# Transposing four looked-up tiles at once, into the PSUM ring of the pieces

## The reference

```python
e = jnp.stack([tbl_0[ids[:, 0]], ..., tbl_31[ids[:, 31]]], axis=1)    # 1024 x 32 x 64
p, q = e[:, ROW], e[:, COL]                                            # ROW, COL: the 496 pairs
kp = jnp.einsum('bpj,ipj->bpi', p, kernel)                             # kernel: 64 x 496 x 64
z = jnp.sum(kp * q, axis=-1)
h = jnp.concatenate([z, dense_ctx], axis=1)
h = jnp.maximum(h @ W_top1 + b_top1, 0.0)                              # 512 x 512
h = jnp.maximum(h @ W_top2 + b_top2, 0.0)                              # 512 x 256
y = h @ W_top3
```

## Time and profile before

| | |
|---|---|
| median of 3 runs | 491.11 us |
| profiled execution | 495.24 us |
| its span, first to last instruction | 493.5 us |
| PE busy | 437.9 us, 89% |
| DVE busy | 301.4 us, 61% |
| ACT busy | 261.4 us, 53% |
| POOL busy | 231.6 us, 47% |
| mean granted TensorE clock | 0.965 |

### The profile page before, as it was taken

How to read it: one execution, slowest core, us unless ns; L and a number is a source line. 1 busy time by engine, 2 the same in 40 slices (tenths; PEclk the granted TensorE clock), 3 DMA queues, 4 the chain that set the end, 5 groups by cost and what they waited for, 6 DMA issues and landing times.

```text
span 493.5 us, 10180 instructions
## 1 busy us (share of the span) xinstructions
PE 437.9 (89%) x3421; PEld 263.6 (53%) x3421; DVE 301.4 (61%) x293; ACT 261.4 (53%) x1874; POOL 231.6 (47%) x251
## 2 busy tenths in 40 slices
PE   8859897978989799798989978987988979999997
PEld 5536464644655555456555645555654646664443
DVE  7407775776747756776666757675668767881000
ACT  6218755754646565645549655460875846601121
POOL 6456566655555645565556555555565530000000
PEclk9867999999999979999999989998999999999999
DMA  5525643121062100211121110301121101000000
GB/s 171 157 64 165 210 109 106 23 62 26 17 166 50 24 18 20 63 23 21 21 66 22 22 23 19 68 18 20 19 65 24 21 18 43 2 1 1 0 1 1
DMA packets 18266, 24.31 MB, mean 49 GB/s; under 512 B 6387, under 2 KB 11767, under 8 KB 17958
## 3 DMA queue, kind: packets, MB, share of 16 engines
q1 hardware_dynamic: 10406, 15.64, 10.8%
q0 software_dynamic: 7808, 8.01, 8.5%
HBM read 19.44 MB, written 0.00 MB: 39 GB/s over the span
## 4 chain that ended last, share of the span: by engine, by line
PE 73%; DVE 7%; another core or an unknown queue 7%; ACT 6%; issue 5%; POOL 0%; DVEq 0%; ACTq 0%; POOLq 0%
PE u_ps L693 30%; PE u_ps L714 12%; PE z_ps L727 10%; DVE prod L610 6%; PE u_ps L774 6%; PE z_ps L733 6%; ACT pass_prod L507 4%; PE t_ps L647 3%; PE u_ps L794 3%; PE u_ps L700 1%; DVE pass_prod L621 1%; PE z_ps L669 1%; ACT rows L495 1%; DVE prod L613 1%
## 5 line engine op out<-in xcount | busy, mean ns | idle before, releaser
L422 POOL DMA_INDIRECT nat<-tbl,ids_sb x244 | 230.5, 945 | 169.8 <-issue 63.0
L610 DVE TENSOR_TENSOR prod<-u_ps,rows 128x1024 f32<-128x1024 f32 x184 | 214.9, 1218 | 105.5 <-PE u_ps L693 71.9
L507 ACT ACTIVATE pass_prod<-pass_prod 128x64 f32<-128x64 f32 x896 | 214.5, 243 | 38.3 <-DVE pass_prod L621 26.5
L693 PE MATMUL u_ps<-rows,k_sb 64*128 64x256 f32 x1472 | 189.3, 395 | 26.8 <-DVE prod L610 10.6
L693 PEld LDWEIGHTS u_ps<-rows,k_sb 64*128 64x128 f32 x1472 | 138.7, 189 | 86.6 <-issue 38.4
L507 ACT ACTIVATION_READ_ACCUMULATOR pass_prod<-pass_prod 128x1 f32 x896 | 169.5, 189 | 2.5 <-issue 2.4
L621 DVE TENSOR_TENSOR pass_prod<-u_ps,nat 128x1024 f32<-128x1024 f32 x56 | 67.7, 1218 | 29.0 <-remote 13.7
L714 PE MATMUL u_ps<-k_sb,rows 64*128 64x256 f32 x448 | 70.0, 437 | 13.8 <-DVE prod L610 11.3
L495 ACT ACTIVATE rows<-t_ps 128x512 f32<-128x512 f32 (+1 forms) x38 | 19.6, 516 | 97.9 <-PE t_ps L647 43.0
L714 PEld LDWEIGHTS u_ps<-k_sb,rows 64*128 64x128 f32 x448 | 44.6, 208 | 34.3 <-DVE prod L610 21.0
L727 PE MATMUL z_ps<-prod,sel 128*32 128x512 f32 x512 | 62.6, 607 | 0.0
(11 more groups left out here) (50 smaller groups left out, 84.1 us busy)
## 6 DMA issues: line engine op xcount, KB each, us to landing
by_self<-rows SPq DMA_DIRECT2D x32, 128.0 KB
nat<-tbl,ids_sb POOLq DMA_INDIRECT x244
k_sb<-kern SPq DMA_DIRECT2D x3, 768.0 KB
k_sb<-kern SPq DMA_DIRECT2D x2, 640.0 KB
k_sb<-kern SPq DMA_DIRECT2D x1, 1152.0 KB
k_sb<-kern SPq DMA_DIRECT2D x2, 512.0 KB
rows<-w SPq DMA_DIRECT2D x1, 1024.0 KB
rows<-tbl SPq DMA_DIRECT2D x4, 224.0 KB
```

The costliest lines, as they stand in the source:

```text
L422: pool.indirect_dma_start(nat_of(m, n)[:, h * EMBED:(h + 1) * EMBED], None, tables[f], bass.IndirectOffsetOnAxis(ids_sb[:, col:col + 1], 0 ...
L507: op = nc.scalar.activation(of, of, ACT.Copy, accum_out=z_nat[:, b % 2, s, row:row + 1])
L610: nc.vector.tensor_tensor(to, u, by.unsqueeze(1).to_broadcast([P, 2, 2, SIZE]), ALU.mult).then_inc(prod_ready, 1)
L693: op = nc.tensor.matmul(u[:, h, :], k_sb[part, k_of(d), side, :], rows[part, tile, cols_of(b)], start=True, stop=True)
```

## The change

Tiles of block 1 and later are transposed four at a time. Their 1024 columns go into an item of the ring `u_ps`, in turn with the pieces (`RING_ITEMS`, `OF_PIECE`, `OF_TILES` hold who has which item); whoever takes an item waits for the one three items before it (`bank_free`), be that a product by DVE or a copy by ACT. ACT copies the four tiles by one instruction. Where a burst has quads and no fold, the four tiles come behind the quads on PE, and behind the copies of `z_ps` on ACT. The look-ups run up to 40 quarter tiles ahead, growing from tile 12 to tile 21. `fold` waits only for the 16 copies of block 0, since `t_ps` is used by nobody else afterwards.

```diff
-AHEAD = 30
+AHEAD, MORE_AHEAD = 30, 10
+def ahead(m):
+    return AHEAD + min(MORE_AHEAD, max(0, m - 11))
 def pieces_in_front(m):
-    return max(0, (4 * m - AHEAD) * (ND + NP) // (4 * TILES))
+    return max(0, (4 * m - ahead(m)) * (ND + NP) // (4 * TILES))
...
     def count(self):
         m = len(self.done)
-        return 2 if m >= TILES and m % 2 == 0 else 1
+        return 4 if m >= TILES else 1
...
+def behind_sums(n):
+    return len(PLAN.quads[n]) > 0 and PLAN.folded[n] is None
...
+RING_ITEMS, OF_PIECE, OF_TILES = [], [], {}
+def take_banks(looked_up):
+    for m, count in looked_up:
+        if m >= TILES:
+            OF_TILES[m] = len(RING_ITEMS)
+            RING_ITEMS.append((None, m + count))
+for n in range(PIECES):
+    take_banks(PLAN.before[n])
+    OF_PIECE.append(len(RING_ITEMS))
+    RING_ITEMS.append((n + 1, None))
+    take_banks(PLAN.behind[n])
...
+        def t_in_ring(m):
+            return u_ps[:, OF_TILES[m] % URING].rearrange("p h s n -> p (h s) n")
...
-                    nc.scalar.activation(rows[:, tile:tile + count, cols_of(b)],
-                                         t_ps[:, 0:count].rearrange("p t n c -> p t (n c)"), ACT.Copy).then_inc(rows_ready, count)
+                    nc.scalar.activation(rows[:, tile:tile + 4, cols_of(b)], t_in_ring(m), ACT.Copy).then_inc(rows_ready, 4)
...
+            def bank_free(item):
+                if item >= URING:
+                    piece, tiles = RING_ITEMS[item - URING]
+                    if piece is not None:
+                        pe.wait_ge(prod_ready, piece)
+                    else:
+                        pe.wait_ge(rows_ready, tiles)
...
+            def transpose_four(m):
+                for t in range(4):
+                    pe.wait_ge(gathered[(m + t) % LANES], lane_count(m + t))
+                bank_free(OF_TILES[m])
+                for t in range(4):
+                    for s in range(SUBS):
+                        op = nc.tensor.transpose(t_in_ring(m)[:, t, s * P:(s + 1) * P], nat_of(m + t, s), ident[:])
+                op.then_inc(transposed, 4)
...
-            def fold(b, tiles):
+            def fold(b):
...
-                pe.wait_ge(rows_ready, tiles)
+                pe.wait_ge(rows_ready, TILES)
...
             def interact(n, b, d):
-                if n >= URING:
-                    pe.wait_ge(prod_ready, n - URING + 1)
+                bank_free(OF_PIECE[n])
...
-                for m, count in PLAN.behind[n]:
-                    transpose(m, count, folds)
-                    tiles += count
+                if not behind_sums(n):
+                    for m, count in PLAN.behind[n]:
+                        if m >= TILES:
+                            transpose_four(m)
+                        else:
+                            transpose(m, count, folds)
+                        tiles += count
                 for quad in PLAN.quads[n]:
                     add_up(quad)
+                if behind_sums(n):
+                    for m, count in PLAN.behind[n]:
...
```

More of the change, by code:

```diff
@@ L170, in landed @@
                 continue
+            if pieces_in_front(n) >= len(self.through):
+                return float("inf")
             self.issued = max(self.issued, self.done[n - RING] if n >= RING else 0, self.through[pieces_in_front(n)]) + 2 * SUBS * GATHER
@@ L239, in in_front @@
         first, last = (next(mark[0] for mark in self.marks if mark[1] == n * (ND + NP)) for n in (1, BLOCKS))
-        due = first + (last - first) / (4 * (LOOKED_UP - TILES)) * (4 * (m - TILES) - AHEAD + part)
+        due = first + (last - first) / (4 * (LOOKED_UP - TILES)) * (4 * (m - TILES) - ahead(m) + part)
         return max(mark for mark in self.marks if mark[0] <= max(0, due))
@@ L291 @@
 PIECES = len(PLAN.order)
+def behind_sums(n):
+    return len(PLAN.quads[n]) > 0 and PLAN.folded[n] is None
 SELFS = [(b, d) for b, d, _ in PLAN.order if d is not None and DOUBLES[d][1] is None]
+assert all(m % 4 == 0 and count == 4 for looked_up in PLAN.before + PLAN.behind for m, count in looked_up if m >= TILES)
 assert PIECES == len(AT) == BLOCKS * (ND + NP) and PLAN.folds == BLOCKS
+RING_ITEMS, OF_PIECE, OF_TILES = [], [], {}
[9 more added lines that the diff above has]
+    take_banks(PLAN.behind[n])
 def tower(nc, ids, first_ids, tables, kern, dense, w1, b1, w2, b2, w3, out):
@@ L558, in _ @@
                     zT_evacuate(PLAN.folded[n])
+                if behind_sums(n):
+                    for m, count in PLAN.behind[n]:
+                        rows_out(m, count)
             z_evacuate(BLOCKS - 1, ZGROUPS - 1)
@@ L630, in _ @@
         def _(pe):
+            def bank_free(item):
[5 more added lines that the diff above has]
+                        pe.wait_ge(rows_ready, tiles)
             def fill(n, count):
-                if count and n >= URING:
-                    pe.wait_ge(prod_ready, n - URING + 1)
+                if count:
+                    bank_free(OF_PIECE[n])
                 for _ in range(count):
-                    nc.tensor.matmul(u_ps[:, n % URING, 0, 0, 0:P], ident[:], ident[:], start=True, stop=True)
+                    nc.tensor.matmul(u_ps[:, OF_PIECE[n] % URING, 0, 0, 0:P], ident[:], ident[:], start=True, stop=True)
             def transpose(m, count, folds):
@@ L713, in interact_pass @@
                         part = slice(EMBED * h, EMBED * (h + 1))
-                        op = nc.tensor.matmul(u_ps[:, n % URING, h, t, :], rows[part, first + t, at:at + P],
+                        op = nc.tensor.matmul(u_ps[:, OF_PIECE[n] % URING, h, t, :], rows[part, first + t, at:at + P],
                                               k_sb[part, k].rearrange("p s n -> p (s n)"), start=True, stop=True)
@@ L759, in _ @@
                     interact_pass(n, b, j)
-                for m, count in PLAN.behind[n]:
-                    transpose(m, count, folds)
-                    tiles += count
+                if not behind_sums(n):
+                    for m, count in PLAN.behind[n]:
+                        if m >= TILES:
+                            transpose_four(m)
+                        else:
+                            transpose(m, count, folds)
+                        tiles += count
                 for quad in PLAN.quads[n]:
                     add_up(quad)
+                if behind_sums(n):
+                    for m, count in PLAN.behind[n]:
+                        if m >= TILES:
+                            transpose_four(m)
+                        else:
+                            transpose(m, count, folds)
+                        tiles += count
                 if PLAN.folded[n] is not None:
-                    fold(PLAN.folded[n], tiles)
+                    fold(PLAN.folded[n])
                     folds += 1
```

16 lines of the change are left out of this document (9 added, 7 removed).

## The result

| | median of the runs, us | ratio to before |
|---|---|---|
| before (same chip) | 492.3 (489.6 to 494.8) | |
| the change | 511.0 (509.4 to 549.6) | 1.037 [1.033, 1.042] |

The change is 3.7% slower, about 18 us; the forecast was 490.5, and its range ended at 500.

What follows compares the result with a forecast made beforehand. The prediction took PE to bound the kernel, so only its idle time or work counts. Its terms, -5.5 + 4.3 + 0.6 + 0 = -0.6 us, lowered a median of 491.1 to 490.5 us, range 482 to 500 us.

Steps and rivals of the forecast that it cites:

- Look-ups: POOL's look-ups for groups of four, released further ahead: rows and ring places come in time, 0 us.
- Waits that come at the two groups right ahead of their pieces: Tiles 20 to 23 and 24 to 27: PE stands 1.26 us plus 0.9 us late signal each, +4.3 us.
- The nine groups behind the sums: Transposes behind the quads: two pieces cover the copy before the third piece needs its item, 0 us.
- the second rival: Slower: ACT, in its own pass sums, copies late and holds a ring item, delaying the third piece; 508 us, chance 0.15.
- the prediction's own sign: PE's waits for ACT's copies summing to over 8 us would show that ACT holds a ring item.
- Waits that go: PE's waits behind passes for two groups (1.67 and 3.54 us) and the second fold's 0.32 us vanish, together -5.5 us.
- The group ahead of its sums: Tiles 36 to 39 need a ring item after four doubles: zero in time, 1.1 us with late signal, +0.6 us.
- Transposes, copies, ACT's queue: As many transposes on PE, ACT's copies of 1.03 us off the path, its queued pass sums wanted later: 0 each.
- Faster, the delays go with the handovers: Half as many groups have half the late signals, halving PE's waits for DVE and ACT: -9.4 us, 482 us, chance 0.25.
- The clock falls at the two groups: Slower: transposes plus waiting at the groups right ahead of their pieces drop PE's clock, 3.2 us each; 497 us, chance 0.05.
- The rule of the Trainium skill on transposes: Transposes don't count as activity for PE's full clock, so eight in a row with a wait are one long pause.
- Look-ups too late for a group of four: Slower: look-ups come too late for a group of four tiles; no size given, chance 0.04.

Runs made afterwards that it cites:

- before_new_pace: The kernel before, with every look-up released where the change releases it (up to 40 quarter tiles ahead): 510.2 us, ratio 1.028.
- after_no_lookups: The change without the look-ups of tiles 20 to 63 and without the waits for them: 446.4 us, ratio 0.918.
- experiment 5: One memset ahead of each look-up from tile 8 on: in the change 508.1 us, in the kernel before with the change's release numbers 505.3 us.
- experiment 1: The kernel before with only the change's release numbers, 510.2 us (1.028); the change with before's numbers for tiles 2 to 19, 514.2 us (1.038).
- no_more_ahead: The change with look-ups released 30 quarter tiles ahead, without the ten more: 511.0 us, ratio 1.035.

## Why the prediction was wrong

**The step that failed** is *Look-ups*: "It fits: 0". It asked only whether the rows are there in time. They are, in the change. It never asked what ten look-ups more do to the signals of PE while they are issued, and it read the trace from 120 us on, where the transposes change, while the release numbers change from tile 7 on, in block 0. With before_new_pace this step measures +14 us (1.028), most of the loss. The forecast's own last sentence named the gap: it only carried the delays of PE's signals over. What it had seen, that they are late while look-ups run and in time after them, was right, and without look-ups DVE starts in time and PE never stands. It was told as a cost that is given, and not followed to what sets it: how closely look-ups follow one another, and for how long. The delay was also sized at PE's waits for DVE alone, 15.1 us; all that the 176 look-ups cost, with other waits, rows of matmuls that stretch and the clock, is 52 us.

**Waits that come at the two groups right ahead of their pieces, +4.3 us.** Right in kind, and a little too high. Without look-ups these waits are 1.27 and 1.26 us, the 1.26 of the sum. In the profiled execution of the change they are 1.26 and 1.27 too (L769 at 161.91, L749 at 182.59): the lower bound of 2.5 us, with no late signal at either.

**The nine groups behind the sums, 0.** Wrong for three of them even without look-ups. The working took the third piece behind a group as the first that needs it. Tiles 28 to 31 are needed by the next piece, tiles 40 to 43 and 56 to 59 by the second, and these three waits are 1.26 and twice 0.24 us in after_no_lookups. With look-ups a part of the second rival came true besides: in the trace of the change PE waits for a copy at six of the nine groups, 1.5 to 2.4 us each and 10.8 of the 12.1 us in all. By the prediction's own sign (over 8 us) the second rival would hold, and it had 17 us. But these waits lie beside waits for DVE: the change lies 2.7 us above the kernel with its release numbers in experiment 5 and 1.0372 - 1.028 = 0.9%, 4.5 us, in experiment 1 (2.0 us by the medians). Both differences are near the noise. So the groups cost some 2 to 5 us together, not 17.

**Waits that go, -5.5 us.** They went, and are inside these 2 to 5 us: the removed ones did not show as a gain of their own.

**The group ahead of its sums, +0.6.** Zero in the trace: PE goes from the burst to the transposes of tiles 36 to 39 without a gap.

**Transposes, copies, ACT's queue: 0.** Right in size: a copy of 1024 columns takes 1.02 us (estimated 1.03), and the eight transposes 1.0 us.

**Rivals.** *Faster, the delays go with the handovers*: refuted; half as many groups, and PE's waits for DVE rose to 18.6 us. *The clock falls at the two groups*: no run isolates transposes, but the clock was already lower where PE stood more, 0.89 instead of 0.93 in the first 120 us, before any group of four. The rule of the Trainium skill on transposes ("TensorE: Matmul & The Clock Gate", Part 4) changed nothing here: in after_no_lookups the stretches with groups of eight transposes keep a granted clock of 1.00. *Look-ups too late for a group of four* had 0.04; no_more_ahead shows that it was the reason for the ten look-ups more, 16.2 us of waits for rows. An upper bound of what look-ups may cost was never made; the rows for it were the earlier trace rows.

**What stays open.** Why a close row of look-ups delays PE's signals, and whether it is the signal that is late or PE's work (the ends of matmuls are modelled, and in the quads of 147.53 PE's own matmuls start late). Length of the pause, number of waits on POOL and pitch went together in the experiments (0.30 us, none and 1.25 us; 0.49, one and 1.43; 0.65, two and 1.60), so which of them lets a signal pass isn't told apart. How the price of k look-ups ahead grows with k, and what it is at the long pitch.

## What to carry to other kernels

A step that lets a producer run further ahead is not free because its results are in time: look at what issuing them does to everybody else, and begin to read where the release changes, not where the work does. Comparing the start of the same piece of work in two traces finds the place of a loss; the sums of waits from 120 us on pointed to the copies (8.4 us more), whose groups cost some 2 to 5 us in all. And leaving the suspected transfers out altogether is the first experiment to make, since it gives the size of the whole (52 us here) before its parts are argued.

## What the runs showed that I had not expected

- Indirect look-ups issued by POOL 1.25 us apart come with signals of PE that DVE, ACT and POOL see 1 to 5 us late; 176 look-ups cost 52 us of 489. The same number of writes on POOL, with the same waits, cost nothing.
- A pause of 0.65 us between all of them takes away most of the delay (0.62 to 0.38 us a product, 0.25 without look-ups); 0.49 us, or 0.65 at every second one, does not.
- Of the kernels that do all look-ups, the one with the best ratio is therefore one with more work: before_gaps, the kernel before with two idle writes ahead of each look-up from tile 20 on, 485.1 us, 0.982 [0.976, 0.988]. It beats both kernels and is limited by POOL's pitch of 1.60 us, with 19 us of waits ahead of transposes.
- While look-ups ran, a pair of quads took 9.4 us instead of 1.9, with gaps where the program has no wait.
- Without look-ups PE has no wait from 120 to 340 us and a granted clock of 1.00 there; with them 24 us of the difference are PE's busy time.
